# Linear attention's scores in four banks at once, with the output projection, the last gates and part of the MLP's output ahead of the products

## What is computed

```python
x = L0_attn_x
xn = _layernorm(x, axis=-1)
s = _L0_attn_ref(xn, ...)          # linear attention, 16 heads of 32
g = _silu(_L0_ffn_ref(xn, ...))    # two layers: window attention and gated MLP
x = x + s * g
```

## Time and profile before

| | |
|---|---|
| median of 3 runs | 2380.59 us (2374.51 to 2381.43) |
| profiled execution, its own time | 2383.1 us |
| its span, first to last instruction | 2381.2 us |
| mean granted TensorE clock | 0.906 |
| PE busy (matmuls) | 2168.9 us, 91% |
| PE weight loads | 1867.6 us, 78% |
| DVE busy | 1827.8 us, 77% |
| ACT busy | 1148.8 us, 48% |
| POOL busy | 934.9 us, 39% |
| chain that ended last | PE 50%, DVE 30%, issue 13% |

### The profile page before, as it was taken

How to read it: one execution, slowest core, us unless ns; L and a number is a source line. 1 busy time by engine, 2 the same in 40 slices (tenths; PEclk the granted TensorE clock), 3 DMA queues, 4 the chain that set the end, 5 groups by cost and what they waited for, 6 DMA issues and landing times.

```text
span 2381.2 us, 48786 instructions
## 1 busy us (share of the span) xinstructions
PE 2168.9 (91%) x15282; PEld 1867.6 (78%) x15282; DVE 1827.8 (77%) x5354; ACT 1148.8 (48%) x2734; POOL 934.9 (39%) x941
## 2 busy tenths in 40 slices
PE   4889989999899989999899989989999999999997
PEld 3778877877787877877787877878888888888786
DVE  5667887778767787688767887777888888888885
ACT  2234443344334443344333443346677676776764
POOL 3334453345434453345433453343333333333331
PEclk8778998889978898899888998889999999999999
DMA  4000000000000000000000000012111111111110
GB/s 162 11 13 17 20 18 14 15 19 18 14 13 19 15 18 14 13 21 18 14 13 15 19 18 14 14 51 69 33 36 33 33 37 32 36 33 33 37 33 25
DMA packets 71792, 64.37 MB, mean 27 GB/s; under 512 B 12444, under 2 KB 64984, under 8 KB 71608
## 3 DMA queue, kind: packets, MB, share of 16 engines
q1 hardware_dynamic: 71736, 63.65, 8.9%
HBM read 38.45 MB, written 12.58 MB: 21 GB/s over the span
## 4 chain that ended last, share of the span: by engine, by line
PE 50%; DVE 30%; issue 13%; DMA 3%; ACT 1%; DVEq 1%; SPq 1%; POOL 1%; POOLq 0%; ACTq 0%
PE bank L1327 38%; PE bank L1332 7%; PE bank L1339 5%; DVE prob L940 4%; DVE prob L926 4%; DMA x_shift<-x 2%; DVE rot L1250 2%; DVE sq_sum L1196 2%; DVE qk_sum L1209 2%; DVE rot L1228 1%; DVE hid L1257 1%; DVE v_mix L1223 1%; DVE mix_work L982 1%; DVE h_n L1158 1%; DVE h_n L1156 1%
## 5 line engine op out<-in xcount | busy, mean ns | idle before, releaser
L1327 PE MATMUL bank<-hT_n,w_s 128*128 128x128 f32 x3072 | 389.6, 279 | 0.5 <-ACT hT_n L711 0.5
L1327 PEld LDWEIGHTS bank<-hT_n,w_s 128*128 128x128 f32 x3072 | 364.9, 193 | 15.2 <-issue 10.8
L1332 PE MATMUL bank<-wqkv_s,xT 128*128 128x512 f32 x1152 | 319.4, 413 | 24.0 <-DVE xT L1104 18.4
L741 ACT ACTIVATE prob<-prob,row_min 128x256 f32<-128x256 f32 x512 | 256.1, 503 | 63.8 <-DVE row_min L926 61.5
L1327 PE MATMUL bank<-w_s,hid 128*128 128x256 f32 x768 | 284.5, 489 | 0.2 <-DVE hid L1257 0.2
L1332 PEld LDWEIGHTS bank<-wqkv_s,xT 128*128 128x128 f32 x1152 | 207.8, 192 | 81.8 <-DVE xT L1104 27.1
L711 ACT ACTIVATE k_dec<-bank 128x512 f32<-128x512 f32 x32 | 19.1, 598 | 515.6 <-PE bank L1339 515.6
L940 DVE TENSOR_SCALAR prob<-prob,row_inv 128x256 f32<-128x256 f32 x512 | 224.3, 480 | 9.2 <-DVE row_inv L935 0.2
L926 DVE CUSTOM_DVE_ANT_0 prob<-bank,table,inv_norm 128x256 f32<-128x256 f32 x512 | 226.2, 478 | 2.7 <-issue 2.7
L633 POOL TENSOR_TENSOR rot_other<-raw,rot_t 128x256 f32<-128x256 f32 x256 | 186.5, 761 | 93.3 <-ACT raw L711 93.3
L596 POOL TENSOR_TENSOR inv_norm<-sq_clip,half_neg 128x16 f32<-128x16 f32 x64 | 188.7, 2948 | 63.6 <-DVE sq_clip L1199 63.6
(11 more groups left out here) (182 smaller groups left out, 4699.8 us busy)
## 6 DMA issues: line engine op xcount, KB each, us to landing
k_prev<-k_carry SPq DMA_DIRECT2D x32, 224.0 KB, 2.5
x_s<-in_L_attn_x SPq DMA_DIRECT2D x32, 128.0 KB, 2.1
rot_s<-in_rotary SPq DMA_DIRECT2D x64, 64.0 KB, 2.0
s_between_passes<-s_out SPq DMA_DIRECT2D x32, 128.0 KB, 1.7
x_between_layers<-x SPq DMA_DIRECT2D x32, 128.0 KB, 1.7
x_s<-x_between_layers SPq DMA_DIRECT2D x32, 128.0 KB, 2.0
xn<-x_between_layers SPq DMA_DIRECT2D x32, 128.0 KB, 2.1
s_out<-s_between_passes SPq DMA_DIRECT2D x32, 128.0 KB, 2.1
```

The lines of the kernel that those rows point to most:

```text
L741: ins = act.activation(prob[:, h, :], prob[:, h, :], ACT.Exp, bias=row_min[:, c:c + 1], scale=-1.0, accum_out=row_sum[:, c:c + 1])
L1327: return pe.matmul(out, lhsT, rhs, start=first, stop=last)
L1332: ins = pe.matmul(out, halved(left[:, a]), halved(right[:, b]), start=first and n == 0, stop=last and n == 2)
```

## The change

Four banks take the four heads' scores: `mix_bank[0]`, `mix_bank[1]`, `att_bank[0]` and `att_bank[2]`. PE issues all scores in one call, g outside and r inside, with no wait for DVE between. In these rounds the window attention's output projection goes to `att_bank[1]`, and PE's next window attention waits for DVE's residual (`x1`) instead of `lb`, as its banks are read until then. After the gates PE does chunks 0 and 1 of the MLP's output ahead of the products; the chunks 2 and 3 follow groups 1 and 3 of the products. On DVE the four `decay_scores` stand together, ahead of q's low part, the residual and the next window's statistics. Rounds without the linear attention keep their order and banks.

```diff
+        score_bank = [mix_bank[0], mix_bank[1], att_bank[0], att_bank[2]]
...
             def decay_scores(mix, r):
-                b = mix_bank[r % 2][:, :].rearrange("p (g i) -> p g i", g=MG)
+                b = score_bank[r][:, :].rearrange("p (g i) -> p g i", g=MG)
...
-            def residual(a):
+            def residual(a, b):
...
-                dve.tensor_tensor(x1[:, a.parity, :], att_bank[2][:, 0:D], res[:, a.parity, :], ALU.add)\
+                dve.tensor_tensor(x1[:, a.parity, :], b[:, 0:D], res[:, a.parity, :], ALU.add)\
                    .then_inc(att_dve.done("x1"), 1)
...
                 if mix is not None:
                     decay_scores(mix, 0)
-                if mix is not None:
                     dve.wait_ge(mix_pool.sem, mix_pool.at("kdec", mix))
                     decay_scores(mix, 1)
+                    dve.wait_ge(mix_pool.sem, mix_pool.at("gate", mix))
+                    decay_scores(mix, 2)
+                    decay_scores(mix, 3)
                 if u is not None:
                     low_turned(u, "qt", "ql", qT, turn_bank(u, 0))
...
                 if a is not None and mix is not None:
-                    residual(a)
+                    residual(a, att_bank[1])
                 if nxt is not None:
                     norm1(nxt)
-                if mix is not None:
-                    dve.wait_ge(mix_pool.sem, mix_pool.at("gate", mix))
-                    for r in range(2, MR):
-                        decay_scores(mix, r)
                 if m is not None and mix is not None:
                     hidden_tail(m)
                 if a is not None and mix is None:
-                    residual(a)
+                    residual(a, att_bank[2])
...
-            def out_projection(a):
+            def out_projection(a, b):
...
-                    ins = mm3(att_bank[2][:, 0:D], oT[:, :, g, :], wo_s[:, :, g, :], g == 0, g == HP - 1)
+                    ins = mm3(b[:, 0:D], oT[:, :, g, :], wo_s[:, :, g, :], g == 0, g == HP - 1)
...
-            def mix_scores(mix, first):
+            def mix_scores(mix):
                 for g in range(MG):
-                    for r in (first, first + 1):
+                    for r in range(MR):
                         rows = slice(r * MD, (r + 1) * MD)
-                        ins = mm(mix_bank[r % 2][:, g * P:(g + 1) * P], kT_mix[rows, g, :], qT_mix[rows, g, :],
+                        ins = mm(score_bank[r][:, g * P:(g + 1) * P], kT_mix[rows, g, :], qT_mix[rows, g, :],
                                  True, True)
...
                     if a.back(1).exists():
-                        pe.wait_ge(att_dve.sem, att_dve.at("lb", a.back(1)))
+                        pe.wait_ge(att_dve.sem, att_dve.at("x1" if i.low <= NW else "lb", a.back(1)))
                     att_scores("a", a, att_bank[0:2])
...
-                    mix_scores(mix, 0)
+                    mix_scores(mix)
                 if a is not None and mix is not None:
-                    out_projection(a)
+                    out_projection(a, att_bank[1])
...
                     hidden(m, mlp_bank[0], 2, 4, 2).then_inc(mlp_pe.done("ga"), 1)
-                if mix is not None:
-                    pe.wait_ge(mix_dve.sem, mix_dve.at("s0", mix))
-                    pe.wait_ge(mix_dve.sem, mix_dve.at("s1", mix))
-                    mix_scores(mix, 2)
                 if a is not None and mix is None:
-                    out_projection(a)
+                    out_projection(a, att_bank[2])
+                if m is not None and mix is not None:
+                    mlp_out(m, 0, 2)
...
                     for g in range(MG):
                         mix_out(mix, g)
-                        if m is not None:
-                            mlp_out(m, g, g + 1)
+                        if m is not None and g % 2 == 1:
+                            mlp_out(m, 2 + g // 2, 3 + g // 2)
```

## The result

| | before | after |
|---|---|---|
| median of the runs | 2381.01 us (4 runs) | 2132.74 us (4 runs, 2131.29 to 2134.0) |
| ratio to before, 95% interval | | 0.896 (0.894 to 0.898) |
| profiled execution, own time / span | 2383.1 / 2381.2 us | 2133.59 / 2131.8 us |
| mean granted clock | 0.906 | 0.983 |

The kernel is 248 us faster, nearly twice the 131 us forecast, and outside the range given. It lies 10 us under the rival "the clock no longer falls" (about 2143).

A forecast was written before the change was run, and what follows sets the result against it. DVE feeds PE up to the oT, then PE's own work sets the time. Per round 2.67 us direct plus 1.8 clock less 0.2 tail is 4.3; thirty rounds plus 3 us take 2383.1 to about 2250 us, range 2205 to 2305.

The forecast's parts named there:

- the clock no longer falls: Rival for the linear-attention rounds: no low clock stretches, 7.9 us gained per round, about 2143 us; chance 0.08.
- All scores at once: PE's score stage: 32 matmuls in four banks take 1.16 us, as 16 did, hidden ahead of DVE's oT.
- The weighing: DVE's weighing of all four score banks in one go takes 2.67 us, so the scores are ready at 846.66.
- Ahead of the products: PE after the gates: two MLP chunks at 0.51 us each cover the wait; products start 1.65 us earlier.
- In the products: PE's product stage: four groups with two chunks instead of four take 5.58 us for 6.60, shortening it by 1.02.
- What is late next: Tail before wout: at the high clock PE's work doesn't quite cover DVE's chain; 0.2 us charged per round.
- a sign of being wrong: Before wout: a new wait of PE above 0.5 us would show the forecast wrong.
- The clock: Product stage: the fall still comes, 3.4 us after the new start; low stretch 8.0 us, not 12.0, gaining 1.8 us.
- The first two rounds: Linear-attention rounds without attention and MLP beside them: only the standstill is saved, 1.5 us each, 3 us in all.
- The unmoved clock: Rival in the products: the clock falls as early as before, low stretch stays 12 us; 83 us gained, 2300; chance 0.21.
- the clock that stays down: Rival in the products and tail: clock low for 24 us, 2.9 us slower per round, 2471 us; chance 0.03.
- The wait that is only moved: Rival ahead of the products: DVE finishes the four banks after PE's cover; time within 0.3% of before; chance 0.03.

The follow-up runs named there:

- filler: The kernel before with three useless 128x256 matmuls per round put into PE's standstill ahead of the products, nothing else changed; 2232.73 us, ratio 0.940.
- banks_only: The kernel after with the two moved MLP chunks put back behind their product groups, scores still in four banks; 2142.93 us (one run).
- chunks_4: The kernel after with all four MLP chunks ahead of the products, so the four product groups stand bare; 2156.96 us (one run).
- wait_tail: The kernel after with PE waiting ahead of the products for DVE's last gates' product, which they don't need; 2248.95 us (one run).
- norm_last: The kernel after with DVE's last step of the next window's norm moved behind the second state addition; 2119.46 us, against 2131.93 for after.
- wait_var: The kernel after with PE waiting ahead of the products until DVE has done the next window's first statistics; 2205.51 us (one run).

## Why the prediction was wrong

**The step that failed** is in the clock: "but the products with 33 columns remain and have less work between them, so I expect the fall, only later". The fall does not come at all. Filler, banks_only and chunks_4 show that the products have no part in it: with the same products, or barer ones, the clock is 1.00 as soon as PE has work in place of the standstill; and wait_tail shows that with the standstill back, in the new order, falls come back. The trace had held this: every fall read came behind the standstill. I took that as a matter of when, and carried the fall over to 3.4 us behind the new start, a number read from a fall whose cause the change removes. So the term of the sum for the clock was 1.8 us per round, where filler shows 4.8. The Trainium skill's rule quoted with the rival (TensorE: Matmul & The Clock Gate, HAM oscillation), that a wait between bursts throttles and joined bursts keep the clock, was right here; the pair of filler and before shows it in its cleanest form. The waits in that section's example are of some 3 to 5 us; here 1.50 was enough, and in this size the measurement decides. I gave that rival 0.08, and its own sum, 2143, was 10 us off.

**Point by point.** *All scores at once:* right, 32 instructions in 1.17 us where 1.16 was taken (the other estimates had been 1.4 and 2.1), and hidden ahead of the oT, for which PE still waits 0.38 us. *The weighing:* right, 2.65 us for 2.67. *Ahead of the products:* the products start 1.89 us earlier, for 1.65: gates and two chunks take 0.89 and 0.87 us instead of 0.98 and 1.02. *In the products:* in filler, groups after the first take 1.55 us at the high clock (867.01 to 868.56), so the full-speed stage of before is 1.65 + 3 x 1.55 = 6.30 us, not 6.60; after takes 5.34, so 0.96 for 1.02. Together 2.85 per round, for 2.67. *What is late next:* right in place, too small: a wait of 0.53 us instead of 0.2, which is also above the 0.5 that the prediction had named as a sign of being wrong; norm_last then won back 0.39 of it. *The clock:* forecast 1.8 us per round; filler's gain is 144 / 30 = 4.8. The bound for no fall had been 5.4, less the tail's wait. *The first two rounds:* 3 us were taken, and 12.7 came (168.31 less 155.58, below).

**Where the 248 us are.** 144 are the clock (filler against before). From filler to after there are 100 more, of which 30 x 2.85 = 86 come directly. (The two make 244; the rest lies between the two medians of before, 2381.01 and 2376.45.) The 14 that are left stand in the first two rounds. The third round's products start so in before, filler and after:

```profile
168.31 0.57 PE L1327 MATMUL bank<-state,qT_dec 128*128 128x132 f32 x2 [1.67 <-DVE mix_work L982]
```

```profile
168.68 0.46 PE L1327 MATMUL bank<-state,qT_dec 128*128 128x132 f32 x2 [0.17 <-DVE mix_work L982]
```

```profile
155.58 0.39 PE L1327 MATMUL bank<-state,qT_dec 128*128 128x132 f32 x2
```

Filler, which puts no work into these two rounds, has gained nothing by then; the kernel after is 13.1 us ahead of it. What in those rounds it comes from, no run takes apart.

**The rivals.** The unmoved clock (0.21) and the clock that stays down (0.03) are both out. The wait that is only moved did not come at this place; the one at wout, 0.53 us in each of 30 rounds, is 16 us, and it comes with the high clock. My forecast's chance of 0.65 stood on a compromise between two causes. A cost between "unchanged" and "gone" did turn up, in wait_tail and wait_var, but there because a wait was left; in the change none was.

## What to carry to other kernels

When the granted clock steps down at the same place in each round, look at the idle time just ahead of the step, and ask what the change does to that wait, not how dense the work is that happens to run slowly afterwards. A wait of 1.5 us that costs 1.5 us on the path cost over 6 here (1.5 and 4.8 for the clock), and even useless work in its place won back the larger part. When moving work ahead to cover a wait, keep enough behind for the next fixed chain: two chunks ahead gained 10 us, and four are 25 us slower than two.

## What the runs showed of the hardware

- PE's waits of 0.87 to 1.50 us took the granted clock from 2.4 to 1.2 GHz for 7 to 14 us, a fall costing 4.5 us of a round in wait_tail. Shorter waits of about 0.97, 0.33 and 0.39 us stand ahead of each of them. The same wait of 1.43 us in the same order did so only in about every second round.
- Shorter waits close together may do it too: in filler the clock fell in 3 of 30 rounds, for 3.4 us each, right behind waits of 0.97 and 0.33 us. No run isolates them, and after has the same two waits in each round and not one fall.
- A run of 40 instructions with 33 or 132 columns, each with a weight load of 128x128 float32, kept the clock at 1.00 for its 4.4 us (chunks_4).
- Four row tiles of 32, each with its own bank, do 32 float32 score matmuls in the time that two tiles take for 16 (1.17 and 1.16 us).
